# Closing matmuls of 64 rows on the two halves of TensorE's rows, and biases added to x, in an eight-core layernorm, scan and ternary-weight layer

## The reference

```python
xn = layernorm(x)                                   # over the last axis, no affine part
a  = tanh(xn @ Wa.T + ba);  b = tanh(xn @ Wb.T + bb)  # 64 channels each
h_t = a_t * h_(t-1) + b_t                           # scan over the 4096 steps
s  = mean(|weight|)
Wt = clip(round(weight / (s + 1e-10)), -1, 1)       # ternary, 2048 x 2048
out = x + (xn + h @ Wout.T + bout) + (xn @ (Wt * s).T + bias)
```

## Time and profile before

| | |
|---|---|
| median of 3 runs | 534.64 us (534.24 to 537.85) |
| the profiled execution: its time | 533.23 us |
| its span (first to last instruction, slowest core) | 531.7 us; 1.53 us lie around it |
| busy: PE, DVE, ACT, POOL | 466.0 (88%), 337.7 (64%), 224.4 (42%), 148.0 us (28%) |
| granted TensorE clock | 1.0 in every slice, core by core 0.999 to 1.000 |
| DMA | 99.14 MB, mean 186 GB/s |

### The profile page before, as it was taken

One profiled execution on the slowest core, in us unless ns is written; L12 is line 12 of the kernel. 1 busy time (PEld: TensorE's weight loads), 2 busy tenths in 40 slices (PEclk: granted clock), 3 DMA queues, 4 the chain that ended last, 5 costly groups with the idle time before them and its releaser, 6 DMA issues.

```text
span 531.7 us, 8044 instructions; the slowest of 8 cores (527.1 to 531.7 us)
## 1 busy us (share of the span) xinstructions
PE 466.0 (88%) x2323; PEld 222.9 (42%) x2323; DVE 337.7 (64%) x515; ACT 224.4 (42%) x210; POOL 148.0 (28%) x388
## 2 busy tenths in 40 slices
PE   0020389999999999999999999999999999999996
PEld 0010135455554545454544444444545454545443
DVE  3533389877787483929494766667675857583643
ACT  0477498565707052443434261707070616252000
POOL 0500037727114050605141322324231415050000
PEclk9999999999999999999999999999999999999999
DMA  7999990472865948594848495857788586844212
GB/s 222 337 327 339 304 257 15 137 182 79 179 198 146 252 120 238 133 199 161 230 153 194 166 199 192 206 191 173 224 149 247 133 264 121 276 119 120 118 43 118
DMA packets 72046, 99.14 MB, mean 186 GB/s; under 512 B 57090, under 2 KB 57090, under 8 KB 65986
## 3 DMA queue, kind: packets, MB, share of 16 engines
q1 hardware_dynamic: 71328, 97.53, 64.5%
q0 software_dynamic: 384, 1.05, 1.3%
q10 hardware_dynamic: 292, 0.05, 0.1%
HBM read 52.48 MB, written 33.55 MB: 162 GB/s over the span
## 4 chain that ended last, share of the span: by engine, by line
PE 60%; DMA 12%; SPq 9%; POOLq 5%; DVE 5%; issue 4%; ACT 3%; DVEq 1%; POOL 0%; ACTq 0%
PE pu L743 47%; DMA sx<-x 6%; DMA wbuf<-wt 6%; PE pu L715 5%; SPq L281 4%; PE pab L702 4%; DVE bst L466 3%; SPq L273 2%; POOLq L882 2%; SPq L286 1%; ACT wbuf L425 1%; POOLq L878 1%; DVEq L468 1%; PE pu L756 1%; PE pu L769 1%
## 5 line engine op out<-in xcount | busy, mean ns | idle before, releaser
L482 DVE SCALAR_TENSOR_TENSOR sx<-pu,scl,sx 128x512 f32<-128x512 f32 x211 | 154.3, 746 | 93.2 <-PE pu L743 43.1
L743 PE MATMUL pu<-wbuf 128*128 128x512 f16 x896 | 204.6, 379 | 0.9 <-issue 0.6
L743 PE MATMUL pu<-wbuf,xnT 128*128 128x512 f16 x672 | 154.2, 379 | 0.9 <-DVE sx L482 0.7
L743 PEld LDWEIGHTS pu<-wbuf 128*128 128x128 f16 x896 | 87.0, 98 | 105.7 <-issue 4.1
L466 DVE BATCH_NORM_STATS2 bst<-sx 128x6 f32<-128x512 f32 x128 | 78.9, 678 | 56.0 <-DMA sx<-x 56.0
L743 PEld LDWEIGHTS pu<-wbuf,xnT 128*128 128x128 f16 x672 | 65.3, 98 | 81.4 <-issue 2.8
L869 POOL TENSOR_SCALAR uu<-mv 128x1 f32<-128x1 f32 (+1 forms) x30 | 9.4, 314 | 236.8 <-DVE mv L470 221.1
L356 ACT ACTIVATE wbuf<-sx,nmr,yr 128x1024 f16<-128x1024 f32 x52 | 61.7, 1231 | 16.6 <-POOLq L891 10.0
L364 ACT ACTIVATE sx<-sx,nmr,p1r 128x2048 f32<-128x2048 f32 x32 | 66.7, 2092 | 2.2
L715 PE MATMUL pu<-wbuf,xnT 128*128 128x512 f16 x240 | 56.4, 379 | 1.2 <-DVE wbuf L587 1.2
L388 ACT ACTIVATE hD<-hs,inv 64x128 bf16<-64x128 f32 x14 | 5.6, 402 | 110.5 <-DVE hs L476 93.5
(11 more groups left out here) (65 smaller groups left out, 301.8 us busy)
## 6 DMA issues: line engine op xcount, KB each, us to landing
sx<-x SPq DMA_DIRECT2D x32, 1024.0 KB, 7.2
y<-sx SPq DMA_DIRECT2D x63, 512.0 KB, 4.3
wbuf<-wt SPq DMA_DIRECT2D x15, 1024.0 KB, 30.6
wbuf<-wt SPq DMA_DIRECT2D x2, 512.0 KB, 34.1
xnT<-wbuf SPq DMA_TRANSPOSE x52, 3.3
wab_s<-wab POOLq DMA_DIRECT2D x1, 512.0 KB, 13.0
y<-sx SPq DMA_DIRECT2D x2, 256.0 KB, 2.5
wocv<-wo POOLq DMA_DIRECT2D x1, 256.0 KB, 15.0
```

The lines of the kernel that those rows point to most:

```text
L482: vector.scalar_tensor_tensor(out, bank(b), scl[:, :], out, OP.mult, OP.add).then_inc(s_ev, 1)
L743: ins = tensor.matmul(bank(b), left(p, lname, c), right(rname, c, h), start=(fresh and c == 0), stop=(state is None and c == HC - 1), skip ...
```

## The change

- `hA` gets 128 rows: the states stand twice, in rows 0 to 63 and in rows 64 to 127 (a second ScalarE copy in `states`). The 65th row is gone, and with it GpSimd's four writes of it and their semaphore.
- Wout lies in `wocq` as 128 x 1024: column quarters q of even number in rows 0 to 63, those of odd number in rows 64 to 127. `mix` multiplies on the rows 64*(q % 2) and following.
- The two column halves of ha0, hb1 and hb0 are closed together, after slot h = 1: two matmuls of 64 rows, one on each half of the rows, in two banks. The unit of h = 0 is signalled there too. In the plain part the units 8 to 15 are closed two by two as well.
- The bias row is summed on VectorE (in partition 0 now), spread over 128 partitions at the start by four TensorE matmuls with one row of ones, and copied from PSUM by ScalarE to `bias` (bf16), between the evictions of tiles 0 and 1 and the third absolute sum. SP's loads of tiles 4 and 5 wait for the last of the four.
- `bias` is added to each x tile after `resid`: on VectorE for tiles 0 and 1 (after its absolute sum number 5), 2 and 3 (in the plain part), and from pair 4 on for 2n+1 after take 4 and for 2n after S4; on GpSimd for tiles 4 to 7, between its chains. `take` and `plain` wait for that addition in place of `resid`.
- `ones` lies in a part of `xnT` that is not yet in use.

```diff
@@ buffers
-        wocv = sb("wocv", [65, D], BF16)
+        wocq = sb("wocq", [128, HD], BF16)
+        bias = sb("bias", [128, D], BF16)
-        hA = sb("hA", [65, 4 * TT], BF16)
+        hA = sb("hA", [128, 4 * TT], BF16)
-        ones = sb("ones", [128, 128], F32)
+        ones = xnT[:, 2 * D:2 * D + 256].bitcast(F32)
@@ sync
-            sync.wait_ge(s_brow, 1)
+            sync.wait_ge(s_bb, 4)
             load(4)
             load(5)
@@ scalar, states(n)
+                scalar.activation(hA[64:128, 2 * i * TT:2 * (i + 1) * TT], hs[:, :],
+                                  AF.Identity, bias=0.0, scale=inv[0:64, :])
                 scalar.activation(hA[0:64, 2 * i * TT:2 * (i + 1) * TT], hs[:, :],
                                   AF.Identity, bias=0.0, scale=inv[0:64, :]
                                   ).then_inc(s_hsb, 1)
@@ scalar, after evict_T(1, 1)
+            for q in range(NQ):
+                scalar.wait_ge(s_bb, q + 1)
+                scalar.copy(bias[:, q * QW:(q + 1) * QW], bank(4)).then_inc(s_bc, 1)
@@ vector
+            def add_bias(t):
+                vector.wait_ge(s_v, POS[t] + 1)
+                if POS[t] == 0:
+                    vector.wait_ge(s_bc, 4)
+                vector.tensor_tensor(xs(t), xs(t), bias[:, :], OP.add).then_inc(s_vb, 1)
...
+            def biased(t):
+                if 4 <= t < 8:
+                    vector.wait_ge(s_vp, t - 3)
+                else:
+                    vector.wait_ge(s_vb, POS[t] + 1 if t < 4 else POS[t] - 3)
...
             for i, c in enumerate(ABS_DVE):
                 absum(c, i, 0, D)
+                if i == 5:
+                    add_bias(0)
+                    add_bias(1)
...
             t3(2)
+            add_bias(2)
             plain(8)
...
             plain(11)
+            add_bias(3)
...
                 take(p, 4)
+                if 3 < n < NP:
+                    add_bias(2 * n + 1)
                 take(p, 5)
...
                 if n < NP:
                     s4(n)
+                if 3 < n < NP:
+                    add_bias(2 * n)
                 take(p, 12)
@@ tensor
+            def mix(b, n, tile, q, skip):
+                lo = 64 * (q % 2)
+                at = (2 * (n % 2) + tile) * TT
+                tensor.wait_ge(s_hsb, n + 1)
+                return tensor.matmul(bank(b), hA[lo:lo + 64, at:at + TT],
+                                     wocq[lo:lo + 64, q // 2 * QW:(q // 2 + 1) * QW],
+                                     start=False, stop=True, skip_group_check=skip)
...
+                elif h == 1:
+                    tile, o = {"ha0": (0, 0), "hb0": (1, 0), "hb1": (1, 1)}[state]
+                    mix(b - 1, p, tile, 2 * o, not fresh).then_inc(s_unit, 1)
+                    mix(b, p, tile, 2 * o + 1, not fresh).then_inc(s_unit, 1)
...
+            for q in range(NQ):
+                if q >= 1:
+                    tensor.wait_ge(s_bc, q)
+                tensor.matmul(bank(4), ones[0:1, :], xs(4)[0:1, q * QW:(q + 1) * QW],
+                              start=True, stop=True).then_inc(s_bb, 1)
@@ gpsimd
-            g.wait_ge(s_inv, 1)
-            for i in range(4):
-                g.tensor_scalar(hA[64:65, i * TT:(i + 1) * TT], ones[64:65, :],
-                                inv[64:65, :], None, OP.mult)
-            g.drain().then_inc(s_hrow, 1)
...
             chain(4, 5)
-            for t in ORD[TURNED:TURNED + 2]:
-                chain(t, t)
+            chain(6, 6)
+            add_bias(4)
+            chain(7, 7)
+            add_bias(5)
...
             g.dma_start(out=wo2[64:128, :], in_=wo_d[:, HD:D]).then_inc(s_wo2, 16)
+            add_bias(6)
+            add_bias(7)
```

More of the change, by code:

```diff
@@ L169, in build @@
         s_inv = sem("s_inv")
-        s_hrow = sem("s_hrow")
+        s_bb = sem("s_bb")
+        s_bc = sem("s_bc")
+        s_vb = sem("s_vb")
+        s_vp = sem("s_vp")
         s_rnd = sem("s_rnd")
@@ L331, in _ @@
             scalar.dma_start(out=bab[:, :], in_=bab_d[:, :]).then_inc(s_bab, 16)
[L332 to L333 removed]
+            scalar.dma_start(out=xs(4)[0:1, :], in_=bo_d[:, :]).then_inc(s_bo, 16)
+            scalar.dma_start(out=xs(5)[0:1, :], in_=bi_d[:, :]).then_inc(s_bi, 16)
             def norm(t):
@@ L717, in plain_part @@
                                   stop=False)
+            def mix(b, n, tile, q, skip):
[5 more added lines that the diff above has]
+                                     start=False, stop=True, skip_group_check=skip)
             def plain_mix(u):
                 t, q = PLAIN[u]
[L721 to L724, removed]
+                mix(PBANK[u], t // 2, t % 2, q, False).then_inc(s_unit, 1)
             def plain(u):
@@ L746, in slot @@
                                         skip_group_check=not fresh)
-                i = p % 2
-                if state is not None:
+                if state is None:
+                    ins.then_inc(s_unit, 1)
+                elif state == "hd":
                     tensor.wait_ge(s_hsb, p + 1)
[L750 to L765, removed]
                     if p == 2:
                         tensor.wait_ge(s_wo2, 32)
[L769 to L773, removed]
+                    i = p % 2
+                    tensor.matmul(bank(b), hD[:, i * TT:(i + 1) * TT],
+                                  wo2[:, h * QW:(h + 1) * QW],
+                                  start=False, stop=True, skip_group_check=not fresh
+                                  ).then_inc(s_unit, 1)
+                elif h == 1:
+                    tile, o = {"ha0": (0, 0), "hb0": (1, 0), "hb1": (1, 1)}[state]
+                    mix(b - 1, p, tile, 2 * o, not fresh).then_inc(s_unit, 1)
+                    mix(b, p, tile, 2 * o + 1, not fresh).then_inc(s_unit, 1)
             tensor.wait_ge(s_idn, 16)
@@ L796, in _ @@
             tensor.wait_ge(s_ad, N_AD)
-            tensor.matmul(pab[:, 256:256 + N_AA + N_AD], ones[:, :], acc[:, :],
+            tensor.matmul(pab[:, 256:256 + N_AA + N_AD], ones, acc[:, :],
                           start=True, stop=True).then_inc(s_sum, 1)
@@ L814, in _ @@
                     gate(0)
[L815 to L817 removed]
+            tensor.wait_ge(s_wol, 32)
             for u in range(NFIRST):
@@ L832, in _ @@
             plain_mix(9)
-            plain(10)
+            plain_part(10, 0, NCH)
             turn(4, 0)
-            plain(11)
+            plain_part(11, 0, NCH)
+            plain_mix(10)
+            plain_mix(11)
             turn(4, 1)
-            plain(12)
+            plain_part(12, 0, NCH)
             turn(5, 0)
-            plain(13)
+            plain_part(13, 0, NCH)
+            plain_mix(12)
+            plain_mix(13)
             turn(5, 1)
-            plain(14)
+            plain_part(14, 0, NCH)
             gate(2)
-            plain(15)
+            plain_part(15, 0, NCH)
+            plain_mix(14)
+            plain_mix(15)
             for p in range(2, NP):
@@ L896, in _ @@
             g.dma_start(out=wab[:, :], in_=wab_d[:, :]).then_inc(s_wabl, 16)
-            g.dma_start(out=wocv[0:64, :], in_=wo_d[:, :]).then_inc(s_wol, 16)
-            g.wait_ge(s_inv, 1)
-            for i in range(4):
-                g.tensor_scalar(hA[64:65, i * TT:(i + 1) * TT], ones[64:65, :],
-                                inv[64:65, :], None, OP.mult)
-            g.drain().then_inc(s_hrow, 1)
+            quarters = wo_d[:, :].rearrange("s (j h w) -> s h j w", h=2, w=QW)
+            for h in range(2):
+                g.dma_start(out=wocq[64 * h:64 * (h + 1), :].rearrange(
+                                "s (j w) -> s j w", j=2),
+                            in_=quarters[:, h, :, :]).then_inc(s_wol, 16)
             chain(2, 2)
```

13 lines of the change are left out of this document (9 added, 4 removed).

## The result

The changed kernel takes 566.56 us (561.64 to 573.67), the kernel before beside it 536.25 us (534.24 to 539.47): ratio 1.0529, 95% interval 1.0429 to 1.0629. A second measurement on another chip gave 565.5 against 532.25 us, ratio 1.0606 [1.0560, 1.0652]. (A ratio compares fast runs with fast runs: in some runs, of either kernel, one half of the chip has a lower granted clock.) The forecast was 552, its range 532 to 563: slower, as forecast, but by the ratios 28 to 32 us slower and not 18. The profiled execution took 566.54 us against 533.23, so its 33.3 us are what has to be explained.

What follows compares the result with a forecast made beforehand. On slow cores the ring of loads (28.0 us) bounds, just above TensorE's pair (27.65). +20 ring, +3 GpSimd, -1.3 tail, -0.5 slack, -3 landings make +18 on 533.23: 551, forecast 552 us, range 532 to 563 (8 in 10).

Steps and rivals of the forecast that it cites:

- the ring: From load of x through statistics, GpSimd's chains, norm and transposes to the next load: 28.0 us a turn on slow cores.
- the lock: GpSimd stands still for the whole of a VectorE addition of two SBUF inputs; 2.16 us where 0.2 to 0.3 is usual.
- GpSimd's additions: Tiles 4 to 7, taken at 5 us each; may hold scan(2) and T4 on VectorE: 3 us once, bounds 0 to 8.
- the order of closings: Column half 0 reported one slot (1.7 us) later, plain units' closings later by one unit at most: free.
- shorter landings: Longer turns spread the loads' bytes more thinly: 0.3 us given back for each of eleven turns, 3 us (bounds 0 and 8).
- The addition for 2n: VectorE's addition behind S4 holds GpSimd's chain for 2m: 2.0 us in each of ten turns, 20 us.
- Rival (4): GpSimd's additions take 10 us or more and VectorE waits for them: 560 to 572 us; chance 0.06.
- TensorE's pair: Couples of 64-row matmuls run side by side: 27.65 us per pair of tiles becomes 27.0 at best, 28.0 at worst.
- The tail: After the last turn TensorE runs free for two pairs, 6 x 0.216: -1.3 us.
- Second copy, start: ScalarE's second copy of the states (0.51 us) is hidden; the start's spread costs zero, up to 4 us.
- rival (2): Loads land near 7.2 us, the ring isn't hit, TensorE sets the pace everywhere: 525 us; chance 0.10.
- rival (3): Couples don't run side by side, the ring unhit; TensorE's pair 27.65 to 28.0: 535 to 540 us; chance 0.04.

Runs made afterwards that it cites:

- e2: Changed kernel with VectorE's addition for 2n moved directly behind that for 2n+1: 553.96 us, ratio 1.0376 to the kernel before.
- e3: Changed kernel with the addition for 2n replaced by four 512-column operations reading PSUM, times 0.0: 550.8 us, ratio 1.0293 to the kernel before.
- e6: Changed kernel, all additions kept, with closing matmuls on all 128 rows: 563.59 us, ratio 1.0529 to the kernel before.
- e1: Changed kernel without GpSimd's four additions (tiles 4 to 7 lack the bias): 555.03 us, ratio 1.0384 to the kernel before.
- e9: Changed kernel without any bias addition, plain units 10 to 15 closed one by one: 535.54 us, ratio 1.0076 to the kernel before.
- e4: Changed kernel without any bias addition, couples, second copy of states and spread kept: 537.88 us, ratio 1.0087 to the kernel before.
- e13: Changed kernel without bias additions, states' matmuls on all 128 rows, every unit closed by itself: 534.43 us, ratio 1.0055 to the kernel before.
- e11: Changed kernel with GpSimd's DMAs for wo2 issued ahead of its addition to tile 5: 564.1 us, ratio 1.0606 to the kernel before.
- e14: Kernel before with only one more copy of the states by ScalarE in each pair: 532.48 us, ratio 1.0003 to the kernel before.
- e7: Kernel before with SP's load of the next 2m+1 issued ahead of the transposes of 2m: 554.3 us, ratio 1.0404.

## Why the prediction was wrong

The direction, the ring and the lock were right. Of the terms of the sum, the largest was about right, one was far too small (GpSimd's additions), one was put at nothing and isn't (the order of closings), and one given back never came (shorter landings).

- **The addition for 2n, +20.** Right in kind: place, length (2.28) and neighbour (2.77 us for a GpSimd operation) are as written. In size I took 2.0 a turn; when it is moved or reads PSUM, the turns 5 to 11 fall by 1.5 (e2) and 1.4 (e3), and e3's time by 13 us against e6. A little smaller in these turns, not larger; in turns 2 to 4 e3 takes off 2.8 a turn, more than its own share.
- **GpSimd's additions, "once, I take 3".** This is the step that failed first. It measured 8 to 12 us, by the ratios and by the turns (e1), where 3 were in the sum and 8 was the bound. The duration was right (4.56 for "5"), and so was what waits for it. What I counted was one wait of up to 5 us; in sum T4's four additions take 13.3 us in place of 4.7, two of them standing directly ahead of the first statistics (8.78 us), and the delay was carried on: turns 2 to 4 are 1.8 us longer each with them than without. Rival (4) named that mechanism and this time, 560 to 572, but put a duration of 10 us or more as its condition. 4.56 was enough, since VectorE's operations queue behind GpSimd's. The Trainium skill (SBUF — State Buffer, "SBUF: two separate sides") has the lock on both sides, for the whole instruction; the rows agree, in both directions (2.77 us for a GpSimd operation, 8.78 for two of VectorE's). The prediction's own reading of it, 4 to 8, was nearer than the 3 that it took.
- **The new order of closings, "free ... the same".** Wrong for the plain units as a step: 2.3 us of the first load's 3.7 (e9 beside e4), and another 1.2 go in e13. The additions ahead of the first load add nothing to this (147.9 with them, 148.1 without, in e4): that term was rightly nothing. Between e4 and e9 the 2.3 us brought only some 0.6 us of time.
- **Shorter landings, -3.** Didn't come. The page's median is 7.2 us before and after. In turn 1 loads landed later, since wo2's DMAs had moved beside them (e11): of a step that moves, its DMAs count, and this one I hadn't followed.
- **TensorE's pair, 27.0.** No: the couples overlap, but 0.42 us against 0.43 gains nothing, so 27.65 stays; neither the 27.0 nor the 28.0 of the worst case. It didn't decide here, with turns of 29 to 33 us. The Trainium skill (TensorEngine Tiling (Array Packing), Key Properties) says that a switch of mode drains the engine; the rows show a cost at each switch, 0.10 us before the couple and 0.1 us behind it, less than the 0.165 that the prediction had for a stream that empties wholly.
- **The tail, -1.3.** From the last load to the end core 1 takes 77.7 us, 77.8 before: nothing, for the same reason.
- **Second copy, start.** The copy is hidden (e14). The start was taken at zero up to 4, and is some 1 us.
- **A slip in the chances.** "Faster by over 1% 0.11" has 0.01 more than rival (2) gives; rival (3), at 535 to 540, lies wholly within 1% or slower.

With the measured sizes: 1.5 x 10 for the ring, 8 to 12 for GpSimd's additions, 3.7 ahead of the first load, no relief: 27 to 31 us, where 28 to 32 were measured. That the 3.7 count in full is argued and not tested: in the changed kernel every turn is the ring's, but e9, which took 2.3 of them off, had turns of 27.7, TensorE's own 27.65. Of turns 2 to 4's excess of 3.6 us, e1 removes 1.8 and e3 2.8; together more than there is. How a late first turn is carried on through the next three, beside the lock, is not settled.

## What to carry to other kernels

Here an addition of two arrays in SBUF on one of VectorE and GpSimd was also a stall, for its whole length, of what the other had queued on arrays in SBUF (not of VectorE's evictions from PSUM): price each by what the other engine has queued in that time, not by its own duration, and count chains of them one behind the other. Before two matmuls are put on the two halves of the array between matmuls on all rows, compare the couple with two full ones in a row, switches included. And where a queue in program order looks too late by a store or a transfer, look for the wait that its present place hides.

## What the runs showed of the hardware

- Two matmuls of 64 rows and 512 columns on different halves end in 0.39 us together and cost the stream 0.42 us between matmuls on 128 rows; two on the same half 0.64 (0.10 ahead and 0.54).
- A GpSimd addition of 128x2048, f32 and bf16, takes 4.56 us and stretches VectorE's f16 additions (T4) from 1.22 us to 3.36 in the mean; evictions of 128x512 with one operand in PSUM keep 0.70 us beside it.
- VectorE's addition of two SBUF arrays (f32 and bf16, 2.28 us) stretches a GpSimd operation on one number per partition from 0.3 to 2.77 us; with one operand in PSUM it doesn't (0.27 and 0.34, e3).
- A load that reuses a buffer waited on its queue 3.8 us (196.40 to 200.19, e7) for the store of 512 KB issued just ahead of it.
